# Expert rows turned by 32x32 blocks: block loads and VectorE in place of TensorE turns in a fused state-space and expert kernel

## The reference

```
xn     = layernorm(x) * gamma + beta
w      = softmax over the 2 best of 8 experts of (xn @ gate_w + gate_b), 0 elsewhere
h[e]   = gelu(xn @ ew1[e] + eb1[e])          # 256 -> 512
moe    = sum_e w[e] * (h[e] @ ew2[e] + eb2[e])  # 512 -> 256, then three rotations
gate   = sigmoid([abel, moe] @ gc_w + gc_b)
out    = layernorm(x + abel * (1 - gate) + moe * gate)
```

## Time and profile before

| | before |
|---|---|
| median of 3 runs | 858.12 us (856.52 to 861.2) |
| the profiled execution | 858.49 us, span 856.7 us |
| PE busy | 681.1 us (80%), 4656 instructions |
| DVE busy | 607.7 us (71%) |
| ACT busy | 440.4 us (51%) |
| POOL busy | 260.6 us (30%) |
| DMA packets, bytes | 81779, 99.16 MB |
| mean granted PE clock | 0.914 |
| expert stage | 515.7 to about 782 us |

### The profile page before, as it was taken

The page is one execution under the profiler, slowest core; times in us unless marked ns, Lnnn a source line. Parts: engine busy times, 40 slices in busy tenths (PEclk is TensorE's granted clock), DMA queues, the critical chain, the costliest instruction groups (busy, mean ns, idle before and its releaser), DMA issues. The chain is left out here.

```text
span 856.7 us, 16114 instructions
## 1 busy us (share of the span) xinstructions
PE 681.1 (80%) x4656; PEld 494.1 (58%) x4682; DVE 607.7 (71%) x1658; ACT 440.4 (51%) x804; POOL 260.6 (30%) x310
## 2 busy tenths in 40 slices
PE   5998489898999999999878877999978999992000
PEld 4784347474655656474647655877766877771000
DVE  5836978798889888897977653666664666662884
ACT  2224374748455564738463425656664656652133
POOL 2001011307153442516063320323321323322662
PEclk9899799999999999999989887999997999997555
DMA  4503315254535363538255322322393222203922
GB/s 124 188 0 106 70 57 101 70 123 150 124 112 112 118 131 105 122 120 215 83 150 188 112 73 78 98 71 72 100 381 125 92 81 74 82 34 109 309 74 98
DMA packets 81779, 99.16 MB, mean 116 GB/s; under 512 B 7728, under 2 KB 71867, under 8 KB 81596
## 3 DMA queue, kind: packets, MB, share of 16 engines
q1 hardware_dynamic: 65308, 68.81, 24.8%
q0 software_dynamic: 16416, 29.67, 14.6%
HBM read 62.42 MB, written 33.68 MB: 112 GB/s over the span
## 5 line engine op out<-in xcount | busy, mean ns | idle before, releaser
L1648 POOL DMA_INDIRECT scratch_ys<-ye,place x78 | 77.8, 997 | 206.4 <-DVE place L1758 134.5
L52 PE MATMUL down<-words,h_s_e 128*128 x936 | 110.8, 274 | 9.4 <-DVE yb L1768 9.2
L52 PE MATMUL bank<-words 128*128 128x512 bf16 (+1 forms) x566 | 107.7, 344 | 9.2 <-DVE words L946 7.5
L52 PE MATMUL up<-xe_s,words 128*128 128x256 bf16 x936 | 112.2, 278 | 3.0 <-DVE xe_s L1784 1.3
L52 PEld LDWEIGHTS down<-words,h_s_e 128*128 128x128 bf16 x936 | 88.5, 97 | 30.2 <-issue 17.7
L52 PEld LDWEIGHTS up<-xe_s,words 128*128 x936 | 90.3, 99 | 21.8 <-issue 9.7
L52 PE MATMUL bank<-mlp_w,shared 128*128 128x256 bf16 x768 | 88.1, 276 | 2.4 <-DVE shared L921 2.4
L460 POOL DMA_INDIRECT scratch_zs<-rows,pos x64 | 74.3, 1161 | 48.5 <-DVE pos L1033 29.7
L52 PE MATMUL bank<-xn_s,mlp_w 128*128 128x512 bf16 x369 | 83.8, 381 | 5.6 <-DVE xn_s L720 4.6
L52 PEld LDWEIGHTS bank<-words 128*128 128x128 bf16 x576 | 55.4, 98 | 56.1 <-DVE words L946 9.1
L52 PEld LDWEIGHTS bank<-mlp_w,shared 128*128 128x128 bf16 x768 | 75.8, 99 | 13.9 <-DVE shared L921 2.9
(11 more groups left out here) (238 smaller groups left out, 1240.6 us busy)
## 6 DMA issues: line engine op xcount, KB each, us to landing
xr<-scratch_zs SPq DMA_DIRECT2D x39, 264.0 KB
words<-scratch_ys SPq DMA_DIRECT2D x16, 514.0 KB, 8.8
scratch_abel<-staged SPq DMA_DIRECT2D x8, 514.0 KB, 3.6
abel_all<-scratch_abel SPq DMA_DIRECT2D x8, 514.0 KB
x_in<-in_x SPq DMA_DIRECT2D x8, 512.0 KB, 5.0
words<-in_out_b_row SPq DMA_DIRECT2D x8, 512.0 KB, 3.4
x_res<-in_mlp_b_row SPq DMA_DIRECT2D x8, 512.0 KB, 3.6
words<-in_x POOLq DMA_DIRECT2D x8, 512.0 KB, 7.6
```

The source lines that it names most:

```text
L52: last = nc.tensor.matmul(dst, lhs(a, k), rhs(b, k), start=start and n == 0, stop=stop and n == total - 1)
L1648: nc.gpsimd.indirect_dma_start(out=ys_dram[:, :], out_offset=bass.IndirectOffsetOnAxis(ap=place[:, k, s:s + 1], axis=0), in_=ye[:, k % 2, ...
```

## The change

Each tile's 256 rows of data are loaded as 32x32 blocks. The tile is seen as 8 row blocks b by 2 halves k by 4 blocks a of channels; the block with rows b and channels (k, a) goes to the partitions of quarter a, at column block (k, b). Inside the block rows are still on partitions. There are eight DMAs per tile, one for each a and k, each of 32 partitions by 8 runs of 32 words (128 bytes), and a ninth DMA for the tags (8 words per row). DVE then turns every 32x32 block in its place with one instruction over 128x512 fp32, into `xt` in SBUF, and with that the whole tile has channels on partitions. The four PE transposes per tile, their PSUM banks and PE's waits for them are gone. ACT's L1681 reads `xt` in place of the PSUM bank. DVE turns two tiles ahead: tiles 0 and 1 before the tails of tile 0, and tile q+2 at the head of body q, before `places`. The semaphore of a load now counts nine DMAs.

```diff
-        xr = sb("xr", [P, 4, ST, ROW])
+        SQ = 32
+        xb = sb("xb", [P, 4, KC, SLOT])
+        tags = sb("tags", [P, 4, ST, ROW - D])
+        xt = sb("xt", [P, 2, KC, SLOT])
...
-        turn_bank = [pb(f"turn{i}", [P, KC, SLOT]) for i in range(2)]
...
-                sp.dma_start(xr[:, k], zs_dram[bass.ds(row, SLOT), :].rearrange("(s p) c -> p s c", p=P))\
+                blocks = zs_dram[bass.ds(row, SLOT), 0:D].rearrange("(b j) (k a i) -> a k j b i", j=SQ, k=KC, i=SQ)
+                for a in range(P // SQ):
+                    for c in range(KC):
+                        sp.dma_start(xb[a * SQ:(a + 1) * SQ, k, c].rearrange("j (b i) -> j b i", i=SQ), blocks[a, c])\
+                            .then_inc(zs_in[k], 16)
+                sp.dma_start(tags[:, k], zs_dram[bass.ds(row, SLOT), D:ROW].rearrange("(s p) c -> p s c", p=P))\
                     .then_inc(zs_in[k], 16)
...
-                    nc.scalar.activation(xe[:, k % 2, c], turn_bank[k % 2][:, c], ACT.Identity, bias=beta[:, c:c + 1],
+                    nc.scalar.activation(xe[:, k % 2, c], xt[:, k % 2, c], ACT.Identity, bias=beta[:, c:c + 1],
...
-                dve.wait_ge(zs_in[k], (q - k) * 4 + 16)
+                dve.wait_ge(zs_in[k], (q - k) * 36 + 144)
...
+            def turned(q, k):
+                dve.wait_ge(zs_in[k], (q - k) * 36 + 144)
+                wait(dve, xe_r, KC * (q - 1))
+                nc.vector.transpose(xt[:, k % 2].rearrange("p k n -> p (k n)"), xb[:, k].rearrange("p k n -> p (k n)"))\
+                    .then_inc(xT_done, 1)
...
                 if isinstance(q, int) and q == 0:
+                    turned(0, 0)
+                    turned(1, 1)
                     tails(0, 0)
+                if not (isinstance(q, int) and q >= QT - 2):
+                    turned(q + 2, (k + 2) % 4)
                 places(q, k)
...
-                if isinstance(q, int) and q == 0:
-                    turned_rows(0, 0)
-                if not (isinstance(q, int) and q == QT - 1):
-                    turned_rows(q + 1, (k + 1) % 4)
                 up(q, k, expert_of(q))
```

More of the change, by code:

```diff
@@ L1742, in tag @@
                 def tag(c, dt):
-                    return xr[:, k, :, c:c + 1].bitcast(dt).rearrange("p s a -> p (s a)")
-                dve.wait_ge(zs_in[k], (q - k) * 4 + 16)
+                    return tags[:, k, :, c - D:c - D + 1].bitcast(dt).rearrange("p s a -> p (s a)")
+                dve.wait_ge(zs_in[k], (q - k) * 36 + 144)
                 wait(dve, ys_out[k], (q - k) * 4 * ST)
@@ L1842, in _ @@
         def _(pe):
[L1843 to L1850, removed]
             def up(q, r, e):
```

## The result

| | before | after |
|---|---|---|
| median of the runs | 859.29 us (856.52 to 861.2, 4 runs) | 874.64 us (872.62 to 875.15, 4 runs) |
| ratio | | 1.0177, 95% interval 1.0142 to 1.0212 |
| the profiled execution | 858.49 us, span 856.7 | 872.62 us, span 870.8 |

A forecast was written before the change was run, and what follows sets the result against it. The prediction took the chain of ACT and DVE steps, 6.40 us per tile, as the bound, not PE. It added 12 (start), 9 (half way) and 3 (ACT from SBUF) to 858.49, giving 882.5 us, range 867 to 908.

The forecast's parts named there:

- The ring of ACT and DVE: Expert stage: the chain of ACT and DVE steps from one bias addition (yb) to the next sets 6.40 us per tile.
- DVE's transposing: Expert stage, each tile: one DVE pass over 128x512 fp32 takes 0.7 us, at no cost per tile.
- the hole named: DVE's idle 1.59 us per tile before the tails at L1784, waiting for ACT, where the transposing would fit.
- ACT from SBUF: L1681 in each tile: 589 ns from SBUF against 550 from PSUM, two per tile, +3.0 us in all.
- The packets: Tile loads: 2304 packets in place of 256, at 1.0 ns each, 2.3 us per tile, hidden beside 6.40.
- Rival 1: Tile loads: short packets cost what 1 KB ones do and bind the loop at 7.9 us per tile, 934 us; chance 0.15.
- rival 2: Tile loads: SP's issuing binds the loop at 6.85 us per tile, 901 us in all; chance 0.10.
- Rival 3: Expert stage: PE was the bound after all, so 22.8 us go and the kernel is faster, 847 us; chance 0.05.
- Rival 4: Tile loads come early enough and nothing is seen but +3 us, 861 us in all; chance 0.07.
- The start: First tiles: nine serial issues per load make the first loads land later, delaying yb of tile 0 by 12 us.
- Half way: Tile 20's load, behind 16 big loads on SP's queue, lands 6.2 us later; with DVE's earlier wait, +9 us.
- Hidden with 3 us to spare: Steady loop: SP needs 5.8 us per tile, and a load lands some 8 us after release, wanted 11.3 later; cost 0.

The follow-up runs named there:

- e_one_turn: Kernel before, with ACT's first step reading the loaded rows in SBUF and three of PE's four turns per tile left out: 859.74 us, ratio 1.003.
- e_act_sbuf: Kernel before, with only ACT's first step reading the loaded rows in SBUF instead of PE's turned copy in PSUM: 861.57 us, ratio 1.005.
- e_nine_pe: Kernel before, PE still turning, with the changed kernel's nine loads per tile into the old buffer: 876.87 us, ratio 1.0208.
- e_longruns: Changed kernel with the same nine DMAs per tile, the eight of data in runs of 1 KB per row: 881.27 us, ratio 1.0282.
- e_ahead1: Changed kernel with DVE turning one tile ahead in place of two: 878.67 us, ratio 1.0243.
- e_onedma: Changed kernel with a tile's data loaded by one DMA of 256 long packets in natural order in place of eight: 865.98 us, ratio 1.0081.

## Why the prediction was right, and where its sizes were off

**What bounds the tile: right.** The ring of ACT and DVE was read link by link out of the earlier trace rows, and the changed kernel has the same links. PE's 96% in the earlier trace rows was no bound (e_one_turn), so taking four turns off it brought 0, as said. This was the choice on which the sign of the forecast rested.

**DVE's transposing: right.** 0.7 us taken, 705 ns measured, in the hole named; 1.08 us of the hole is left, where under 1 was forecast.

**ACT from SBUF: right.** +3.0 forecast; the ring went from 6.40 to 6.48 in e_act_sbuf alone and in the changed kernel, and the 37 ordinary gaps took 3.2 us more.

**The packets: right in kind.** 1.0 ns each was interpolated and 0.90 measured for 128 bytes (0.84 with the tags' packets), 2.0 us per tile where 2.3 was forecast, beside 6.48; the DMA engines' busy share in the stretch of the earlier trace rows went from 0.25 to 0.44 and nothing in the ring waited for it. The Trainium skill (DMA: Bandwidth & Descriptors, Specifications), which gives 512 B as the least transfer for line rate, is borne out by the trace as far as it goes: 128 bytes in 0.90 ns are 142 GB/s, and the packets of 1056 bytes of the kernel before, in the stretch of the earlier trace rows, took 3.77 ns, which is 280 GB/s. Whether that matters is read from the loop: a load's packets fill 2.0 us of a tile's 6.48. Rival 1 is out, and rival 2 too for this kernel (a load takes SP 5.1 us at the start and 5.8 on the mean of loads 4 to 13, and from load 14 on SP waits for place). Rival 2 was nearer than its chance says: e_nine_pe, e_longruns and e_ahead1 took 6.5 us per load over the same tiles, as long as the ring. Rival 3 is out by e_one_turn. Rival 4 is out by the start.

**The start: right mechanism, mis-sized.** 12 forecast, 9.7 measured (8.3 between the two runs with spread loads, mostly by the clock at the first product). The term that was too large is the price of an issue, 0.57 us. The earlier trace rows give 378 ns for a DMA of 128 partitions; the new ones of 32 partitions take 317 ns, so they stand 0.50 us apart and a load takes 5.1 us, not 5.8. That is 1.7 us at the landing of load 3 (22.9 us behind the first issue; 24.6 forecast), and the way from there to yb of tile 0 was 3.7 us, not the 4.7 that I laid out by hand.

**Half way: right mechanism, mis-sized.** 9 forecast, 6.1 measured as the difference of the gaps, 6.8 as the delay of yb of tile 18 over that of tile 0 with 0.08 for each of the 14 ordinary tiles taken off. Tile 20 landed 5.0 us later, where 6.2 was forecast. Of the two terms in the 6.2 both came close: load 19 held SP 4.2 us longer (4.6), and load 20 took 1.7 us longer from its first issue to its first use (1.6). Two others were not in the sum: place of tile 15 came 0.6 later, behind the transposing, and SP got to load 20 in 1.5 us less after load 19; 1.0 of it is that the 16 big loads went out faster. And yb of tile 18 followed the landing by 10.4 us against 8.6 before, 1.8 more and not 2.8. That part, DVE's wait a tile earlier, e_onedma pays as well (1.8 of its 3.7). The 8.6 itself holds matmuls at the lower clock: up took 4.71 us there and 2.79 in the ring. The prediction has no clock in it.

**What was not in the sum.** "Hidden with 3 us to spare" took SP to be on time in the loop. It was 5 us behind at load 4 and caught up only at load 14. In the changed kernel that did no harm, by 5 tiles of margin before the big loads. In e_nine_pe, e_longruns and e_ahead1 SP had not caught up by load 19, and the arrears of the start were paid a second time half way. This is the largest part of what all three missed their expectations by. The same paragraph puts the issue at which SP would be even with the ring at 0.42 us; by its own terms it is (6.40 - 0.64) / 9 - 0.19 = 0.45.

**From the stage to the median.** The stage grew by 18.9 us and the medians by 15.35. The profiled pair has its 4.8 us from stage one, whose end lies between 510.96 and 515.73 us over the thirteen profiles, though no run edits it. Of the 8 us by which 882.5 was too high, 5.1 are the terms (24 against 18.9) and the rest lies between the profiled executions and the medians; no run says why stage one varies.

## What to carry to other kernels

Before an engine at 96% is relieved, add up the links from one repeat of a step to the next: if the sum comes out without it, relieving it brings nothing, and any extra cost of the new path is the whole effect. Count DMA instructions per transfer as a serial cost on the queue that issues them; it shows where the queue has no head start (the first tiles) and wherever a block of other transfers stands in the same queue, and in these runs arrears made in one place were paid again in the next. A block of big loads in front of a small urgent one is worth spreading before anything else: that edit alone gave 7 us here. And before a difference of 1 or 2 us between two traces is explained, look at the granted clock where each gap ends: one product at the lower level costs 1.3 to 2.5 us more here.

## What the runs showed of the hardware

- An issue on SP takes 317 ns for a DMA over 32 partitions and 378 ns for one over 128 (390 for the tags), with an address in a register; with the register instructions between them nine stand 0.50 us apart.
- Issues are not all alike: single ones in the changed kernel take up to 1.52 us (the tags of load 3, 530.91), and while SP was behind it took 5.4 to 6.4 us per load of nine in the changed kernel and 5.5 to 7.7 in e_nine_pe. No run tells what holds them.
- A DMA of 32 rows of 1 KB is no easier for SP than one of 256 runs of 128 bytes: the first three loads of nine take 4.5, 4.4 and 4.4 us to issue in e_longruns and in the changed kernel.
- A packet of 128 bytes took 14.3 ns of one DMA engine, 0.90 ns of the 16; one of 1056 bytes 60 ns, 3.8 of the 16 (kernel before); one of 1 KB 86 ns, 5.4 of the 16, in e_longruns.
- While PE waited in the stalls the granted clock fell from 1.00 to 0.50, and the 24 matmuls of up behind them took 4.1 to 5.3 us in place of 2.79.
- DVE turns the 32x32 blocks of 128x512 fp32 in 705 ns, about the price of its ordinary operation with two inputs of that shape (684 to 692 ns).
- ACT's operation of 128x256 takes 585 to 587 ns from SBUF and 550 from PSUM, the only difference in the ring.
